# Entering the layers of a small transformer: the last norm, the copy of x, the norm's move into x, the rotation tables and the first weight product in one block

## The reference, cut to what matters

```python
def _layernorm(x, axis=-1, eps=1e-05):
    m = jnp.mean(x, axis=axis, keepdims=True)
    v = jnp.var(x, axis=axis, keepdims=True)
    return (x - m) / jnp.sqrt(v + eps)
...
    x = x + _L1_attn_ref(_layernorm(x, axis=-1), ...)
    x = x + _L1_ffn_ref(_layernorm(x, axis=-1), ...)      # six layers inside
...
        for i in range(DEPTH):
            x = attn_layer(shift_tokens(x), Wqkv[i], q_scale[i], k_scale[i], Wo[i]) + x
            x = ffn_layer(shift_tokens(x), ln_g[i], ln_b[i], W1[i], b1[i], W2[i], b2[i]) + x
        return x
```

## Time and profile before

| what | us |
|---|---|
| median of 3 runs | 3930.85 (3927.55 to 3932.21) |
| the profiled execution's own time | 3925.54 |
| its span, first to last instruction | 3923.7 |
| PE busy in it | 3752.4 (96%) |
| DVE, ACT, POOL busy | 3199.5, 2779.9, 2574.1 |
| mean granted TensorE clock | 0.99 of 2.4 GHz |

### The profile page before, as it was taken

One profiled execution on the slowest core, in us unless ns is written; L12 is line 12 of the kernel. 1 busy time (PEld: TensorE's weight loads), 2 busy tenths in 40 slices (PEclk: granted clock), 3 DMA queues, 4 the chain that ended last, 5 costly groups with the idle time before them and its releaser, 6 DMA issues. The chain is left out here.

```text
span 3923.7 us, 156108 instructions
## 1 busy us (share of the span) xinstructions
PE 3752.4 (96%) x61563; PEld 2392.6 (61%) x61579; DVE 3199.5 (82%) x5483; ACT 2779.9 (71%) x6389; POOL 2574.1 (66%) x2467
## 2 busy tenths in 40 slices
PE   7997898999999999999999999999999999999998
PEld 4665684666655666646666556666466665566664
DVE  6886556899967999868999779999589997699996
ACT  6984215888846888748888568887388885588883
POOL 4553334788836888737888458887278885488882
PEclk9999998999999999999999999999999999999999
DMA  2000000000000000000000000000000000000001
GB/s 77 0 0 1 1 0 1 1 5 0 0 23 3 0 5 0 1 24 1 0 5 0 23 3 0 5 0 1 24 1 0 5 0 23 3 0 5 0 1 44
DMA packets 12428, 28.26 MB, mean 7 GB/s; under 512 B 2460, under 2 KB 6728, under 8 KB 11344
## 3 DMA queue, kind: packets, MB, share of 16 engines
q1 hardware_dynamic: 12240, 25.72, 1.9%
HBM read 23.62 MB, written 2.10 MB: 7 GB/s over the span
## 5 line engine op out<-in xcount | busy, mean ns | idle before, releaser
L979 POOL TENSOR_TENSOR w_t<-w_t 128x512 f32<-128x512 f32 x768 | 979.4, 1285 | 413.5 <-DVE w_t L1320 413.5
L1320 DVE TENSOR_TENSOR w_t<-banks,w_tab 128x512 f32<-128x512 f32 x1536 | 956.0, 684 | 237.7 <-ACT w_sq L1450 228.9
L995 POOL TENSOR_TENSOR w_t<-w_t,w_rn 128x512 f32<-128x512 f32 x768 | 784.4, 1042 | 251.7 <-ACT w_rn L1492 251.7
L1095 PE MATMUL banks<-w_qk,w_xs 128*128 128x512 f32 x1536 | 826.2, 620 | 10.5 <-issue 9.4
L1115 PE MATMUL banks<-w_vo,w_xs 128*32 128x256 f32 x12288 | 823.3, 385 | 4.9 <-ACT w_us L1443 4.9
L1103 PEld LDWEIGHTS banks<-ident,w_t 128*128 128x128 f32 x3072 | 380.2, 140 | 424.1 <-issue 405.0
L1443 ACT ACTIVATE w_us<-banks 128x512 f32<-128x512 f32 x768 | 456.8, 595 | 162.4 <-PE banks L1115 157.8
L1103 PE MATMUL banks<-ident,w_t 128*128 128x128 f32 x3072 | 461.1, 273 | 18.6 <-POOL w_t L995 10.5
L1115 PEld LDWEIGHTS banks<-w_vo,w_xs 128*32 128x32 f32 x12288 | 321.8, 109 | 243.5 <-issue 78.0
L1360 DVE TENSOR_REDUCE w_ss<-w_sq 128x16 f32<-128x1024 f32 x384 | 465.0, 1211 | 0.0
L1154 PE MATMUL banks<-w_us,w_prT 128*32 128x128 f32 x10752 | 410.5, 273 | 22.4 <-issue 17.7
(11 more groups left out here) (178 smaller groups left out, 6051.1 us busy)
## 6 DMA issues: line engine op xcount, KB each, us to landing
w_qk<-w_qk_in SPq DMA_DIRECT2D x7, 1024.0 KB, 4.8
w_v<-w_v_in SPq DMA_DIRECT2D x7, 512.0 KB, 5.6
w_o<-w_o_in SPq DMA_DIRECT2D x7, 512.0 KB, 6.4
m_w<-m_w_in SPq DMA_DIRECT2D x6, 342.0 KB
xT<-x_in SPq DMA_DIRECT2D x4, 512.0 KB, 5.7
out<-kept SPq DMA_DIRECT2D x8, 256.0 KB, 2.4
m_w<-m_w_in SPq DMA_DIRECT2D x6, 171.0 KB
r_tab<-r_tab_in SPq DMA_DIRECT2D x1, 512.0 KB
```

Source lines behind the costliest of these rows:

```text
L979: nc.gpsimd.tensor_tensor(v1, v1, v2[:, :, ::-1, :], ALU.add).then_inc(S["added"], 1)
L995: nc.gpsimd.tensor_tensor(v1, v1, rn[j % 2][:, i * HALF:(i + 1) * HALF].unsqueeze(2) .broadcast_to([P, HALF, WD]), ALU.mult).then_inc(S["n ...
L1095: nc.tensor.matmul(banks[:, i, :], x[:], wqk[:, i * INNER + hh * C:i * INNER + (hh + 1) * C], start=True, stop=True).then_inc(S["qk"], 1)
L1320: nc.vector.tensor_tensor(dst[j % 2][:, i * C:(i + 1) * C].rearrange("p (h d) -> p h d", d=WD), src, tab[:, 2 * t + cs, i * WD:(i + 1) * W ...
```

## The change

The three pieces (norm, small block, prelude of `layers`) become one block, `enter_layers`. The subtraction, squares, variances, Ln and Exp stay. DVE gets a copy of x into `kept` right behind each subtraction, and its scale now writes straight into `xT`, so ACT's eight copies (L187) are gone. DVE makes the tables ahead of its first subtraction. PE runs the 16 fuse products behind the last variance, into four banks, with no wait inside; ACT takes the first two groups behind its last Exp, and DVE the other two behind its last scale. `w_vo` is allocated in the program and handed in.

```diff
-    layer_norm(nc, sem, 3, xT, norm, logv, mean_w, eps_col, banks)
-
     kept = sb("kept", [P, B, T])
-    moved = sem("moved")
-    with nc.Block() as block:
-        @block.vector
-        def _(dve):
-            for b in range(0, B, PER):
-                nc.vector.tensor_copy(kept[:, b:b + PER, :], xT[:, b:b + PER, PAD:PAD + T]).then_inc(moved, 1)
-
-        @block.scalar
-        def _(act):
-            for b in range(0, B, PER):
-                act.wait_ge(moved, b // PER + 1)
-                nc.scalar.activation(xT[:, b:b + PER, PAD:PAD + T],
-                                     norm[:, b * T:(b + PER) * T].rearrange("p (b t) -> p b t", b=PER), ACT.Copy)
+    w_vo = sb("w_vo", [P, WH, P])
+    enter_layers(nc, sem, xT, norm, logv, mean_w, eps_col, banks, kept, w_v, w_o, w_vo, w_base, w_scl, w_tab)
...
-            pe.wait_ge(S["weights"], 64)
-            fuse(0, 0)
-            fuse(0, 1)
             with pe.Fori(0, DEPTH) as layer:
...
-            dve.wait_ge(S["weights"], 64)
-            tables()
-            take_fused(0)
             with dve.Fori(0, DEPTH) as layer:
...
-            take_fused(0)
             with act.Fori(0, DEPTH) as layer:
```

More of the change, by code:

```diff
@@ L171, in program @@
     retention(nc, sem, xT, norm, logv, banks, ident, eps_col, r_w, r_wv, r_wg, r_wo, r_gn, r_tab, r_decay, r_hm)
-    layer_norm(nc, sem, 3, xT, norm, logv, mean_w, eps_col, banks)
     kept = sb("kept", [P, B, T])
-    moved = sem("moved")
-    with nc.Block() as block:
-        @block.vector
-        def _(dve):
-            for b in range(0, B, PER):
-                nc.vector.tensor_copy(kept[:, b:b + PER, :], xT[:, b:b + PER, PAD:PAD + T]).then_inc(moved, 1)
-        @block.scalar
-        def _(act):
-            for b in range(0, B, PER):
-                act.wait_ge(moved, b // PER + 1)
-                nc.scalar.activation(xT[:, b:b + PER, PAD:PAD + T],
-                                     norm[:, b * T:(b + PER) * T].rearrange("p (b t) -> p b t", b=PER), ACT.Copy)
-    layers(nc, sem, h, xT, norm, logv, banks, ident, w_qk, w_v, w_o, w_base, w_scl, w_tab, w_mask, m_w1, m_w2, m_col)
+    w_vo = sb("w_vo", [P, WH, P])
+    enter_layers(nc, sem, xT, norm, logv, mean_w, eps_col, banks, kept, w_v, w_o, w_vo, w_base, w_scl, w_tab)
+    layers(nc, sem, h, xT, norm, logv, banks, ident, w_qk, w_v, w_o, w_vo, w_base, w_scl, w_tab,
+           w_mask, m_w1, m_w2, m_col)
     stored, summed = sem("stored"), sem("summed")
@@ L841, in layers @@
 @scoped
-def layers(nc, sem, sb, h, xT, spare0, spare1, banks, ident, wqk, wv, wo, base, scl, tab, mask, w1, w2, col):
+def layers(nc, sem, sb, h, xT, spare0, spare1, banks, ident, wqk, wv, wo, wvo, base, scl, tab, mask, w1, w2, col):
     N = B * STEPS
@@ L846, in layers @@
     xs = [sb(f"w_xs{t}", [P, P]) for t in range(TILES)]
-    wvo = sb("w_vo", [P, WH, P])
     sq = sb("w_sq", [P, 2, HALF, WD])
@@ L1539, in one_layer, with enter_layers, chunk, of @@
                 gelu(NCH - 1, 1, 2)
-            take_fused(0)
             with act.Fori(0, DEPTH) as layer:
                 one_layer(layer)
+def enter_layers(nc, sem, xT, norm, logv, mean_w, eps_col, banks, kept, wv, wo, wvo, base, scl, tab):
+    mean_in, centred = sem("ln_mean"), sem("ln_centred")
+    squared, var_in, logged = sem("ln_squared"), sem("ln_var"), sem("ln_logged")
+    inverse, scaled = sem("ln_inverse"), sem("ln_scaled")
+    moved, weights, tabled = sem("moved"), sem("w_weights"), sem("w_tabled")
+    fused, taken0, taken1 = sem("w_fused"), sem("w_fused_taken0"), sem("w_fused_taken1")
+    done = NCH * 3
+    def chunk(buf, c):
+        return buf[:, c * CH:(c + 1) * CH]
+    def of(buf):
+        return buf.rearrange("p (b t) -> p b t", b=PER)
+    def stream(c):
+        return xT[:, c * PER:(c + 1) * PER, PAD:PAD + T]
+    def fused_bank(part, par):
+        return banks[:, 2 * part + par, :].rearrange("p (g n) -> p g n", n=P)
+    def fused_weights(part, par):
+        return wvo[:].rearrange("p (u g a) n -> p u a g n", u=2, a=2)[:, part, par]
+    with nc.Block() as block:
+        @block.tensor
+        def _(pe):
+            def variance(c):
+                pe.wait_ge(squared, passed(done + c + 1))
+                nc.tensor.matmul(banks[:, c, :], mean_w[:], chunk(logv, c), start=True, stop=True).then_inc(var_in, 1)
+            for c in range(NCH):
+                nc.tensor.matmul(of(banks[:, c, :]), mean_w[:], stream(c), start=True, stop=True).then_inc(mean_in, 1)
+                if c >= BEHIND:
+                    variance(c - BEHIND)
+            for c in range(NCH - BEHIND, NCH):
+                variance(c)
+            pe.wait_ge(weights, 64)
+            pe.wait_ge(logged, passed(done + 4))
+            for part in range(2):
+                for par in range(2):
+                    rows = slice(64 * par, 64 * par + 64)
+                    for g in range(4):
+                        last = nc.tensor.matmul(fused_bank(part, par)[:, g], wv[rows, part * 4 + g, :],
+                                                wo[rows, part * 4 + g, :], start=True, stop=True)
+                    last.then_inc(fused, 1)
+        @block.vector
+        def _(dve):
+            def scale(c):
+                dve.wait_ge(inverse, passed(done + c + 1))
+                dve.wait_ge(centred, passed(done + c + 1))
+                dve.wait_ge(moved, c + 1)
+                nc.vector.tensor_tensor(stream(c), of(chunk(norm, c)), of(chunk(logv, c)), ALU.mult).then_inc(scaled, 1)
+            dve.wait_ge(weights, 64)
+            nc.vector.tensor_tensor(tab[:], base[:], scl[:].unsqueeze(1).broadcast_to([P, 2 * TILES, 2 * WD]),
+                                    ALU.mult).then_inc(tabled, 1)
+            for c in range(NCH):
+                dve.wait_ge(mean_in, passed(done + c + 1))
+                nc.vector.tensor_tensor(of(chunk(norm, c)), stream(c), of(banks[:, c, :]), ALU.subtract)\
+                    .then_inc(centred, 1)
+                nc.vector.tensor_copy(kept[:, c * PER:(c + 1) * PER, :], stream(c)).then_inc(moved, 1)
+                if c >= 2 * BEHIND:
+                    scale(c - 2 * BEHIND)
+            for c in range(NCH - 2 * BEHIND, NCH):
+                scale(c)
+            for par in range(2):
+                dve.wait_ge(fused, passed(2 + par + 1))
+                nc.vector.tensor_copy(fused_weights(1, par), fused_bank(1, par)).then_inc(taken1, 1)
+        @block.gpsimd
+        def _(pool):
+            for c in range(NCH):
+                pool.wait_ge(centred, passed(done + c + 1))
+                nc.gpsimd.tensor_tensor(chunk(logv, c), chunk(norm, c), chunk(norm, c), ALU.mult).then_inc(squared, 1)
+        @block.scalar
+        def _(act):
+            nc.scalar.preload_act_table_set("natural_log_exp_and_others")
+            for c in range(NCH):
+                act.wait_ge(var_in, passed(done + c + 1))
+                nc.scalar.activation(chunk(logv, c), banks[:, c, :], ACT.Ln, bias=eps_col[:]).then_inc(logged, 1)
+                act.wait_ge(logged, passed(done + c + 1))
+                nc.scalar.activation(chunk(logv, c), chunk(logv, c), ACT.Exp, scale=-0.5).then_inc(inverse, 1)
+            for par in range(2):
+                act.wait_ge(fused, passed(par + 1))
+                nc.scalar.activation(fused_weights(0, par), fused_bank(0, par), ACT.Copy).then_inc(taken0, 1)
```

## The result

The changed kernel takes 3908.98 us (median of 5 runs, 3906.67 to 3913.03), the one before 3929.83 (5 runs, 3927.55 to 3932.21). The ratio is 0.9949, 95% interval 0.9934 to 0.9963: 20.9 us faster, where 3.8 were forecast. The range began at 3920.5.

The account below looks back on a forecast made before the run. PE, busy 96% of the span, bounds the kernel; only layer 1's first product moves. Summed from the last square, it starts 3.54 to 3.98 us earlier, taken as 3.8: 3930.85 - 3.8 = 3927.0 us, range 3920.5 to 3933.0.

Parts of the forecast that it names:

- a chain that should shift as a whole: Everything behind layer 1's first product was to move earlier unchanged, so only that product's start, 645.81 us before, counted.
- a sign of being wrong: Layers 2 to 6 should be unchanged to within 1 us each; the prediction is wrong if the layers themselves change.
- a rival, but only as a loss: Layer loops' code lands elsewhere, doubling PE's idle gaps at loop turns: 16.7 us more, 12.9 net, 3943.8; chance 0.06.
- The fuse: PE's fuse products straight behind the last variance, ahead of layer 1: 5.88 us at 1.2 GHz.
- my other end: The whole fuse at the full clock, 3.42 us, from half a fuse taking 1.71.
- fast fuse: Rival: the fuse ahead of layer 1 runs at full clock, saving 2.46 more, 6.3 us in all, 3924.6; chance 0.16.
- The collision: Norm's late chunks: DVE's copy then scale queue against POOL's square; rounds 2.26 to 2.37, last square losing 1.25 to 1.69 us.
- the longer end: In the norm's late chunks the copy blocks POOL's square as a scale does: rounds of 2.37, 1.69 us lost.
- The table load: Table load and first shift, hidden beside the fuse before, now uncovered ahead of layer 1's first product: 1.94 us on the path.
- The tables: DVE's tables, 0.69 us, ahead of its first subtraction, hidden because that cannot start before about 615.8.
- The first products of layer 1: They stay at 1.2 GHz, since PE is idle for 3.3 us ahead of them.

Follow-up runs that it names:

- allback: Changed kernel plus semaphore increments (13 ACT, 4 DVE, 3 PE, 3 POOL) putting every engine's layer loop where it stood before: 3919.18 us, 6.4 below before, ratio 0.9983.
- dmacopy: Changed kernel with the eight copies into `kept` made by DMA from SP's queue, eight semaphore increments keeping DVE's code in place: 3907.66 us, ratio 0.9957 to before.
- dmatable: The changed kernel with copies into `kept` by DMA and ACT's table load moved from each layer's start to its end: 3905.85 us, ratio 0.9953 to before.

## Why the prediction was wrong, point by point

- **"What lies behind it is a chain that should shift as a whole"** is the step that failed. Behind the first product 10 us of the span went that the sum has no term for; by the medians the places of the code gave 12. Each of the first five layers became more than 1 us shorter, which the prediction had named as a sign of being wrong. The 6.4 us of the new block alone would have given 3923.4, within the range. I had read the idle time "without a wait" at the loop's turns and had the mechanism as a rival, but only as a loss, with a chance of 0.06, and let it go because PE's list "loses only a few waits". The gaps that it counted (1.09 and 1.70) are not the one that shrank, which is that ahead of each layer's first product (1.83 and 1.93). Three entries fewer on PE were enough, and four on DVE. The two lines of instruction transfers on the page were not read.
- **The fuse.** I took 5.88 from a fuse that began on a slow clock. Here it began on a full one, at 633.26, and the clock held to its end: 2.82. 3.42 was my other end, from two halves in a later layer. The 3.1 us are what lies between the 3.5 forecast for the first product and the 6.5 measured. allback measures this part of the change by itself as 6.4; the rival "fast fuse" had 6.3, with 0.16.
- **The collision** was right in place, order and size: rounds of 2.40, 2.37 and 2.38 for 2.26 to 2.37, scales of 1.53. The square takes 1.15 beside a copy and 1.04 without one, so the copy holds POOL up for 0.11, as the longer end had it. dmacopy gives 1.8 as the price, just above the 1.25 to 1.69.
- **The table load** on the bare path was right: 1.28 and the shift 0.64 lie between 637.26 and 639.19. dmatable won 1.0 of the 1.28.
- **The tables** ahead of the first subtraction were hidden, since the first subtraction starts at 616.29. The first products of layer 1 ran slow again (3.17 for 3.75), but not as forecast: the granted clock was still 1.00 through the 3.3 us of idle time, and fell to 0.50 only 0.6 us into the products. In dmacopy they take 3.75.

## What to carry to other kernels

A handful of instructions ahead of a loop can move its code across a border of what an engine reads again in each pass, and that can be worth more than the edit that brought them. It cost time here also on PE, which read code in every layer on either side of the border. Before crediting an edit with a gain inside code that it doesn't touch, look at the page's instruction transfers and at the idle time at the loops' turns, and put the old places back with padding. A copy that fits into an engine's idle time by its length can still cost a round where another engine's operation queues between it and the next.

## What the runs showed that I had not expected

- Two to four semaphore increments of 0.1 to 0.15 us move the whole kernel by 9 to 12 us, with the same work on every engine.
- The costs of two engines' stalls don't add: 12 and 9 alone, 12 together, because DVE's fetch is over before the later PE needs it.
- ACT's 26 transfers more cost 1.4 us, within the spread of the runs; DVE's 25 cost 9, of which some 5 are its late starts and the rest goes with a lower clock of PE.
- Products as small as the fuse's kept the full clock for all of 2.82 us when they found it so, while 5.88 us of them had not raised it.
